# Interleaving half a batch of transposes with one finish, and issuing stores one tile at a time

## What is computed

```python
def step(x, wb):
    wi, bi = wb
    xw = jnp.matmul(x, wi)
    return x0 * xw + bi + x, None
x, _ = jax.lax.scan(step, x0, (w, b))
```

## Time and profile before

| | |
|---|---|
| runs, median (lowest to highest) | 1411.83 us (1409.92 to 1413.0) |
| profiled execution, span | 1412.7 us |
| VectorE busy | 1151.1 us, 81% |
| TensorE busy (matmul) | 694.4 us, 49% |
| ScalarE busy | 95.6 us, 7% |
| bytes moved | 537.63 MB, mean 381 GB/s |

### The profile page before, as it was taken

The page is one execution under the profiler, slowest core; times in us unless marked ns, Lnnn a source line. Parts: engine busy times, 40 slices in busy tenths (PEclk is TensorE's granted clock), DMA queues, the critical chain, the costliest instruction groups (busy, mean ns, idle before and its releaser), DMA issues.

```text
span 1412.7 us, 20472 instructions
## 1 busy us (share of the span) xinstructions
PE 694.4 (49%) x8724; PEld 662.6 (47%) x8724; DVE 1151.1 (81%) x529; ACT 95.6 (7%) x324; POOL 7.2 (1%) x32
## 2 busy tenths in 40 slices
PE   7455455364454553553544544535436445455352
PEld 4445455354454453553544544535435445455352
DVE  4879788878788797787887877878878878779777
ACT  1000000000000000000000000000000000000000
POOL 2000000000000000000000000000000000000000
PEclk9777676777676776766766767667677777677776
DMA  9999999999999999999999999999999999999956
GB/s 318 372 407 387 386 397 394 395 401 388 392 389 383 381 401 394 383 386 391 389 381 394 386 387 383 392 385 387 393 387 391 387 388 386 390 379 393 392 244 263
DMA packets 38016, 537.63 MB, mean 381 GB/s; under 512 B 4254, under 2 KB 4446, under 8 KB 5470
## 3 DMA queue, kind: packets, MB, share of 16 engines
q1 hardware_dynamic: 18716, 269.13, 49.8%
q10 hardware_dynamic: 19296, 268.44, 47.1%
HBM read 269.12 MB, written 268.44 MB: 381 GB/s over the span
## 4 chain that ended last, share of the span: by engine, by line
DVE 61%; issue 20%; PE 7%; ACT 6%; ACTq 2%; DVEq 1%; DMA 1%; SPq 0%
DVE blocks L267 40%; DVE tiles L280 20%; PE turned L364 7%; ACT spread L197 5%; ACTq L209 2%; ACT growth L202 1%; DMA tiles<-in_L_rec_w_dram 1%; DVE scale L274 1%; PE dots L350 1%; DVEq L289 1%; DVE tiles L314 1%; ACTq L201 0%; ACTq L192 0%; DVEq L279 0%; DVEq L272 0%
## 5 line engine op out<-in xcount | busy, mean ns | idle before, releaser
L350 PE MATMUL dots<-blocks,weights 128*64 128x128 f32 x8192 | 585.8, 316 | 466.8 <-DVE blocks L267 466.1
L350 PEld LDWEIGHTS dots<-blocks,weights 128*64 128x64 f32 x8192 | 570.2, 165 | 473.0 <-DVE blocks L267 472.0
L280 DVE SCALAR_TENSOR_TENSOR tiles<-tiles,scale,c_last 128x4096 f32<-128x4096 f32 x126 | 562.5, 4464 | 0.0
L267 DVE STREAM_TRANSPOSE blocks<-tiles 128x2048 f32<-128x2048 f32 x252 | 559.7, 2279 | 0.0
L274 DVE TENSOR_TENSOR_SCAN scale<-growth,cw 128x6 f32<-128x6 f32 x128 | 15.7, 164 | 244.5 <-ACT growth L202 244.5
L364 PE MATMUL turned<-layer_sel,spread 128*128 128x8 f32 x512 | 92.5, 308 | 227.9 <-ACT spread L197 227.9
L364 PEld LDWEIGHTS turned<-layer_sel,spread 128*128 128x128 f32 x512 | 86.6, 255 | 243.3 <-ACT spread L197 243.3
L197 ACT ACTIVATE spread<-dots,group_mask 128x128 f32<-128x128 f32 x256 | 73.0, 368 | 1179.0 <-DVE tiles L280 1168.4
L202 ACT ACTIVATE growth<-turned,ones 128x16 f32<-128x16 f32 x64 | 17.5, 273 | 103.8 <-PE turned L364 103.8
L242 DVE STREAM_TRANSPOSE blocks<-tiles 128x1024 f32<-128x1024 f32 x8 | 9.2, 1210 | 8.8 <-DMA tiles<-in_r_inputs_dram 8.8
L332 PE MATMUL scratch<-tiles,ones 6*128 6x512 f32 x16 | 14.4, 1076 | 2.0 <-ACT c_last L187 2.0
(11 more groups left out here) (18 smaller groups left out, 5.3 us busy)
## 6 DMA issues: line engine op xcount, KB each, us to landing
tiles<-in_r_inputs_dram SPq DMA_DIRECT2D x128, 2048.0 KB, 11.3
out_dram<-tiles ACTq DMA_DIRECT2D x126, 2048.0 KB, 9.6
out_dram<-tiles ACTq DMA_DIRECT2D x8, 512.0 KB, 3.1
tiles<-in_L_rec_w_dram SPq DMA_DIRECT2D x4, 96.0 KB
strips_b<-in_L_rec_b_dram SPq DMA_DIRECT2D x1, 96.0 KB, 2.0
strips_w<-in_L_rec_w_dram SPq DMA_DIRECT2D x1, 96.0 KB, 2.0
tiles<-in_L_rec_b_dram SPq DMA_DIRECT2D x1, 96.0 KB
```

Of the source, the lines that this page charges most:

```text
L267: nc.vector.transpose(blocks[:, c, :, :].rearrange("p t n -> p (t n)"), tiles[:, q * TB:(q + 1) * TB, c * CH:(c + 1) * CH]).then_inc(block ...
L280: nc.vector.scalar_tensor_tensor(out=tiles[:, s, :], in0=tiles[:, s, :], scalar=scale[:, q % 2, t, L - 1:L], in1=c_last[:], op0=ALU.mult, ...
L350: last = nc.tensor.matmul(dots[at:at + KM * Q, :, :, :], weights[:, c * KB + k:c * KB + k + KM, :], blocks[:, c, :, k * Q:(k + KM) * Q], s ...
```

## The change

On VectorE, the order for batch b becomes: wait for the two loads of b; transposes of chunks 0 and 1 of b; scans of b-1; finish of the first tile of b-1; transposes of chunks 2 and 3 of b; finish of the second tile of b-1. On ScalarE, it becomes: store the first tile of b-1; spreads of b; store the second tile of b-1; growth of b. The loops of SyncE, ScalarE and VectorE are written out by Python, so these engines have no run-time loop. TensorE's program, the buffers and the last batch's pieces are the same.

```diff
-            with sp.Fori(1, n_rounds) as r:
-                for s in range(n_slots):
-                    sp.wait_ge(y_stored[s], r * 16)
-                    sp.dma_start(tiles[:, s, :], x[bass.ds((r * n_slots + s) * P, P), :]).then_inc(x_landed[s], 16)
+            for n in range(n_slots, n_tiles):
+                s = n % n_slots
+                sp.wait_ge(y_stored[s], n // n_slots * 16)
+                sp.dma_start(tiles[:, s, :], x[n * P:(n + 1) * P, :]).then_inc(x_landed[s], 16)
...
-            make_growth(0, first=True)
-            for q in range(1, BR):
-                store(q - 1, 0, q - 1)
-                make_growth(q)
-            with act.Fori(1, n_rounds) as r:
-                store(r * BR - 1, r - 1, BR - 1)
-                make_growth(r * BR)
-                for q in range(1, BR):
-                    store(r * BR + q - 1, r, q - 1)
-                    make_growth(r * BR + q)
+            def store(n):
+                act.wait_ge(tiles_done, n + 1)
+                act.dma_start(out[n * P:(n + 1) * P, :], tiles[:, n % n_slots, :]).then_inc(y_stored[n % n_slots], 16)
+
+            spread_dots(0)
+            make_growth(0)
+            for batch in range(1, n_batches):
+                store((batch - 1) * TB)
+                spread_dots(batch)
+                store((batch - 1) * TB + 1)
+                make_growth(batch)
...
-            def transpose_and_finish(batch, q, landed, last=False):
-
-                for s in range(q * TB, (q + 1) * TB):
-                    dve.wait_ge(x_landed[s], landed)
-                for c in range(NCHUNK):
-                    dve.wait_ge(blocks_used, (batch - 1) * NCHUNK + c + 1)
-                    transpose_chunk(batch, q, c)
-                finish(batch - 1, (q - 1) % BR, TB - 1)
-                scan(batch, q)
-                for t in range(0 if last else TB - 1):
-                    finish(batch, q, t)
...
+            for batch in range(1, n_batches):
+                for n in range(batch * TB, (batch + 1) * TB):
+                    dve.wait_ge(x_landed[n % n_slots], (n // n_slots + 1) * 16)
+                transpose_chunks(batch, range(0, NCHUNK // 2))
+                if batch == 1:
+                    dve.wait_ge(scratch_copied, n_halves)
+                    dve.wait_ge(cw_ready, 1)
+                scan(batch - 1)
+                finish(batch - 1, 0)
+                transpose_chunks(batch, range(NCHUNK // 2, NCHUNK))
+                finish(batch - 1, 1)
+            scan(n_batches - 1)
```

More of the change, by code:

```diff
@@ L189, in _, with spread_dots @@
             nc.scalar.copy(cw[:], cw_all[:]).then_inc(cw_ready, 1)
-            def make_growth(batch, first=False):
+            def spread_dots(batch):
                 act.wait_ge(blocks_used, (batch + 1) * NCHUNK)
-                if first:
+                if batch == 0:
                     act.wait_ge(group_mask_ready, 1)
@@ L198, in make_growth @@
                                          scale=group_mask[:, g:g + 1]).then_inc(dots_spread, 1)
+            def make_growth(batch):
                 act.wait_ge(turned_ready, batch + 1)
-                if not first:
+                if batch > 0:
                     act.wait_ge(scale_ready, batch * TB)
@@ L264, in _, with transpose_chunks @@
                 transpose_tile(t)
[L266 to L271, removed]
+            def transpose_chunks(batch, chunks):
+                at = batch * TB % n_slots
+                for c in chunks:
+                    dve.wait_ge(blocks_used, (batch - 1) * NCHUNK + c + 1)
+                    nc.vector.transpose(blocks[:, c, :, :].rearrange("p t n -> p (t n)"),
+                                        tiles[:, at:at + TB, c * CH:(c + 1) * CH]
+                                        ).then_inc(blocks_ready, 1)
@@ L272, in scan, with finish @@
+            def scan(batch):
                 dve.wait_ge(growth_ready, batch + 1)
                 for t in range(TB):
-                    nc.vector.tensor_tensor_scan(scale[:, q % 2, t, 0:L], growth[:, t, 0:L], cw[:, 0:L],
+                    nc.vector.tensor_tensor_scan(scale[:, batch % 2, t, 0:L], growth[:, t, 0:L], cw[:, 0:L],
                                                  1.0, ALU.mult, ALU.add).then_inc(scale_ready, 1)
-            def finish(batch, q, t):
-                s = q * TB + t
+            def finish(batch, t):
+                s = (batch * TB + t) % n_slots
@@ L279, in finish @@
                 dve.wait_ge(scale_ready, batch * TB + t + 1)
                 nc.vector.scalar_tensor_tensor(out=tiles[:, s, :], in0=tiles[:, s, :],
-                                               scalar=scale[:, q % 2, t, L - 1:L], in1=c_last[:],
+                                               scalar=scale[:, batch % 2, t, L - 1:L], in1=c_last[:],
                                                op0=ALU.mult, op1=ALU.add).then_inc(tiles_done, 1)
-            def transpose_and_finish(batch, q, landed, last=False):
-                for s in range(q * TB, (q + 1) * TB):
-                    dve.wait_ge(x_landed[s], landed)
-                for c in range(NCHUNK):
-                    dve.wait_ge(blocks_used, (batch - 1) * NCHUNK + c + 1)
-                    transpose_chunk(batch, q, c)
-                finish(batch - 1, (q - 1) % BR, TB - 1)
-                scan(batch, q)
-                for t in range(0 if last else TB - 1):
-                    finish(batch, q, t)
@@ L314, in _ @@
                 nc.vector.scalar_tensor_tensor(out=tiles[:, s, at], in0=tiles[:, s, at],
-                                               scalar=scale[:, (BR - 1) % 2, t, L - 1:L], in1=c_last[:, at],
+                                               scalar=scale[:, (n_batches - 1) % 2, t, L - 1:L], in1=c_last[:, at],
                                                op0=ALU.mult, op1=ALU.add).then_inc(tiles_done, 1)
```

## The result

The changed kernel takes 1286.51 us (median of four runs, 1286.09 to 1289.64) against 1411.81 beside it: ratio 0.9118, 95% interval 0.9105 to 0.9131. The forecast was 1325 in a range of 1272 to 1400. The profiled execution has a span of 1285.0 us and took 1286.89.

What follows compares the result with a forecast made beforehand. VectorE's period with its wait for growth was the bound, then the transfers: 537.63 MB at 411 GB/s gives 1308 us, plus 8 at the start and 9 at the end, 1325 us, range 1272 to 1400.

Steps and rivals of the forecast that it cites:

- The wait for growth on VectorE's chain was the bound: VectorE's batch period included a 4.14 us wait for ScalarE's growth, 244.5 us in all; the new order removes it.
- The bound passes to the transfers, and VectorE waits some 2 us a batch for loads: In the batch loop, VectorE could run at 18.1 us a batch, so transfers bound it, with periods of 20 to 21 us.
- nearly five transfers are under way where now about two are: In the batch loop, VectorE's later finishes and stores leave more loads and stores in flight at once.
- I take the middle, 411: Rate per full DMA share for all transfers, between 393 and 429 GB/s, giving 1308 us.
- switching loss: Between loads and stores: a transfer in the other direction waits for the current one to drain slowly.
- The head: First 60 us: 9.8 us lost against the transfer rate, of which 8 were expected to remain.
- the last 65 us: Kernel's end: 33 us after the last landing, with about 9.9 MB of stores worth 24 us, so 9 lost.
- the three terms: Whole kernel: transfers 1308 us, start loss 8 us and end loss 9 us, together 1325 us.
- rival C: Transfers: switching loss disappears, both directions always flow at 429 GB/s; 1270 us, chance 0.12.
- The ends: Start and end of the kernel: losses outside the steady transfers, 8 and 9 us, 17 in the rivals' sums.
- so no gain: Loops of SyncE, ScalarE and VectorE written out: loop steps are fractions of a microsecond that vanish in waits.
- Rival D: Transfers: deeper mixing makes slow windows more frequent, 377 GB/s and 1445 us; share already 0.99 spoke for it; chance 0.09.

Runs made afterwards that it cites:

- e2: Kernel before with loops written out and only ScalarE's new order (one store before the spreads, one behind), VectorE's order old: 1290.91 us, ratio 0.9131.
- e3: Kernel before with loops written out and only VectorE's new order; ScalarE still issues both stores before the spreads: 1286.2 us, ratio 0.9143.
- e1: Kernel before, old order on VectorE and ScalarE, with only the loops of SyncE, ScalarE and VectorE written out: 1384.71 us, ratio 0.980.
- e5: Changed kernel's order on VectorE and ScalarE, but with run-time loops on SyncE, ScalarE and VectorE as before: 1287.51 us, ratio 0.9112.
- e6: Changed kernel with two more transposes a batch on VectorE into a spare buffer: 1447.85 us, ratio 1.0245 against the kernel before.
- The copy: Loads and stores alone, all arithmetic left out; against the kernel before: eight slots 1252.33 us, ratio 0.8864; four slots 1252.35 us, 0.8861.
- two-slot copy: Loads and stores alone with two slots, all arithmetic left out: 1333.88 us, ratio 0.9438 against the kernel before.

## Why the prediction was right, and where it was off

*The wait for growth on VectorE's chain was the bound.* Right, and shown by taking it away in two ways that have only the written-out loops in common (e2, e3), whose own worth is known (e1) and which aren't needed (e5). More work on VectorE makes it the bound again (e6). The dots ended 3.2 us after the last transpose in the period shown, within the 3.4 reckoned; growth had 4.9 us to spare there, where 1.8 were reckoned: it came 1.5 us after the finish and not 2.6, mainly because the eight small matmuls took 1.06 us and not 1.87, and 1.95 us are the wait for loads.

*The bound passes to the transfers, and VectorE waits some 2 us a batch for loads.* Right: 1.95 us each (109.2 / 56), with a period of 19.8 us where 20 to 21 were written. From the end of the last wait for loads to the end of the span it is 35.0 us, where 33 were reckoned. Of ScalarE's waits only part came as written: the spreads now wait for the dots (1057.1 us in 63 waits), and 24.4 us in 15 waits for a finish are left in front of the growth.

*"... nearly five transfers are under way where now about two are."* The number is about right (4.1), the reason isn't. The prediction derived it from the new order on VectorE. But e2 has 4.6 with the old order, and e6 has 2 x 21.4 / 22.1 = 1.9 with the new one (8.39 MB at 379 GB/s are 22.1 us). The transfers pile up because they are the bound, whichever order made them so.

*"I take the middle, 411."* This term was mis-sized, and it carries nearly all of the error of 40 us. The middle of the kernel runs at 425 GB/s at a share of 1.01 (425 / 1.01 = 421 per full share, as the prediction counts it), so most of the switching loss vanished: 537.69 MB / 425 = 1265 us, against 1308. The argument against it was that four transfers under way "is not many". The copy shows that four are enough for 431 and two are not. The number of transfers, nearly five, had been worked out; what was missing was a row that said from how many on nothing is lost. The head was worth 60 - 21.8 MB / 425 = 8.7 us against 8, and the last 65 us 65 - 22.5 / 0.425 = 12 against 9. With 425 in place of 411 the sum is 1265 + 8.7 + 12 = 1286. That this meets the span of 1285.0 is no test, as the three terms are that span taken apart; it shows where the 40 us lie. The measured rate lies between the forecast's 411 and rival C's 429, and nearer to C. So is the time: 16 us above C's 1270 and 39 below the forecast's 1325, at the edge of the forecast's own range (1285 to 1365). C had been given a chance of 0.12 and the forecast 0.52, so the bound was foreseen and the size of its rate was not. The ends, 17 us in both, were 4 us too few.

*Loops: "so no gain".* Not so on the old chain, where they cost 27 us (e1), right for the changed kernel, where a wait covers them (e5). The gaps of 0.1 to 0.2 us between ScalarE's instructions in the earlier trace rows were read as fractions that vanish in waits; but they stand between the finish and the growth that VectorE waits for. Over the batches they make 15 us, and as much follows behind them.

*Rival D.* The share of 0.99 as a sign that transfers had no room: e6 shows that share stays at 0.97 with VectorE as the sole bound.

*One reading is not settled.* That the slow stretches are the draining of one direction before the other starts fits and the windows of the two-slot copy. But that copy lost 6%, less than the kernel before, with as many microseconds in which one queue moves alone (about 920 of 1160). Nor is it shown why a transfer waits. Part of it is a start-up of its own: at the start of the two-slot copy, with nothing else under way, the first packet comes 1.0 us after the first load's issue, and in its middle 2.6 us after a load's and 2.5 after a store's (medians). The rest may be the draining of the other direction; no run separates the two, nor the change of direction from the small number of transfers as such.

## What to carry to other kernels

When a busy share of the DMA engines is near one, look at what they move in that share: if the same share carries 324 GB/s in one window and 429 in another, there is room, and more transfers under way may take it. Look too whether both directions move in the same microseconds or take turns. Before costing an engine's wait, ask who stands in front of the releaser in its own queue; a store whose tile isn't ready can hold up everything that its issuing engine has to compute. Small steps of a sequencer cost as many times as the chain passes them, and only while that chain is the bound.

## What the runs showed that was not expected

- A store took 25.5 us to land and a load 14.9 in the fastest kernel, 9.7 and 11.7 in the slowest (e6): the time of one transfer says little of the rate of all.
- The copy took the same time with four slots as with eight (1252.35 and 1252.33).
- Half of each finish left out was worth 3 us of 1286, for 255 us less of VectorE's time in the middle stretch.
